# Gathers of the edge passes: a wait before every pair on the pair two back, in place of a wait before every run of four

## The reference

```python
m = jnp.concatenate([hc[row], hc[col]], axis=1)
m = jax.nn.silu(m @ w1 + b1)
m = jax.nn.silu(m @ w2 + b2)
agg = jax.ops.segment_sum(m, row, num_segments=N) * C
```

```python
m_j = norm[:, None] * x[from_]
out = jax.ops.segment_sum(m_j, to_, num_segments=n)
```

## Time and profile before

| | |
|---|---|
| median of 3 runs | 12680.3 us (12676.23 to 12695.34) |
| profiled execution | 12673.93 us, its span 12672.1 us |
| POOL busy | 7744.8 us, 61% of the span |
| PE busy | 9185.8 us, 72% |
| DVE busy | 5764.2 us, 45% |
| ACT busy | 2483.4 us, 20% |
| gathers of `edge_messages` (L1210) | 4160, mean 1014 ns |

### The profile page before, as it was taken

How to read it: one execution, slowest core, us unless ns; L and a number is a source line. 1 busy time by engine, 2 the same in 40 slices (tenths; PEclk the granted TensorE clock), 3 DMA queues, 4 the chain that set the end, 5 groups by cost and what they waited for, 6 DMA issues and landing times. The chain is left out here.

```text
span 12672.1 us, 187503 instructions
## 1 busy us (share of the span) xinstructions
PE 9185.8 (72%) x45085; PEld 7667.0 (61%) x45086; DVE 5764.2 (45%) x14751; ACT 2483.4 (20%) x4616; POOL 7744.8 (61%) x7547
## 2 busy tenths in 40 slices
PE   3774488777887777777777777999996667774333
PEld 2663244466766666566666666888885556664333
DVE  9773000034333333333333334888888733333223
ACT  0000233300011000100010001555554611110000
POOL 5556777666655666566656664555553456665776
PEclk5555689866666666666666666999998967775555
DMA  1332244421113111311121112888886412221111
GB/s 28 101 109 67 85 145 138 125 48 44 43 37 73 44 43 44 66 43 44 43 57 43 44 43 77 254 254 253 254 253 169 127 48 51 52 51 28 25 25 25
DMA packets 854760, 1110.03 MB, mean 88 GB/s; under 512 B 337331, under 2 KB 531544, under 8 KB 853398
## 3 DMA queue, kind: packets, MB, share of 16 engines
q1 hardware_dynamic: 306058, 473.67, 13.0%
q0 software_dynamic: 264160, 418.34, 12.0%
q10 hardware_dynamic: 284332, 215.58, 6.6%
HBM read 898.41 MB, written 208.50 MB: 87 GB/s over the span
## 5 line engine op out<-in xcount | busy, mean ns | idle before, releaser
L1210 POOL DMA_INDIRECT gx_l<-xr,gi_l x4160 | 4219.5, 1014 | 2475.5 <-DMA gx_l<-xr,gi_l 1155.2
L1332 DVE TENSOR_TENSOR pre_s_l<-psum,gx_l 128x512 f32<-128x512 f32 x520 | 359.7, 692 | 3251.6 <-DMA gx_l<-xr,gi_l 3251.6
L1375 PE MATMUL psum<-ptab,oht 128*128 x6656 | 1288.5, 374 | 405.3 <-issue 333.6
L1375 PEld LDWEIGHTS psum<-ptab,oht 128*128 128x128 f32 x6656 | 1216.1, 282 | 517.7 <-issue 517.7
L1902 PE MATMUL psum<-cw,xa 128*128 128x256 f32 x6656 | 1503.4, 382 | 26.7 <-DVE xa L1988 24.5
L1319 DVE TENSOR_TENSOR aggT_l<-aggT_l,psum 64x128 f32 x4160 | 1157.1, 278 | 755.6 <-DVE aggT_l L1319 724.5
L1890 POOL DMA_INDIRECT gx<-xr,gi x832 | 899.4, 1081 | 969.1 <-DVEq L1979 467.7
L1902 PEld LDWEIGHTS psum<-cw,xa 128*128 128x128 f32 x6656 | 1237.6, 191 | 231.0 <-issue 75.3
L926 POOL DMA_INDIRECT slots_s<-rec_s,row_s x806 | 815.1, 1011 | 590.7 <-issue 339.4
L1223 PE MATMUL psum<-ident,pre_s_l 128*128 128x128 f32 x2080 | 379.2, 312 | 939.2 <-DVE pre_s_l L1332 939.0
L2512 POOL DMA_INDIRECT gx_l<-xr,gi_l x832 | 823.5, 990 | 321.4 <-issue 162.0
(11 more groups left out here) (374 smaller groups left out, 12380.3 us busy)
## 6 DMA issues: line engine op xcount, KB each, us to landing
wkv<-slots_d ACTq DMA_DIRECT2D x208, 568.0 KB, 6.7
kr<-keyrow_s SPq DMA_DIRECT2D x416, 256.0 KB, 3.1
shb<-shT SPq DMA_DIRECT2D x1664, 64.0 KB
gx_l<-xr,gi_l POOLq DMA_INDIRECT x4992, 2.4
vtab<-kv ACTq DMA_DIRECT2D x208, 256.0 KB
v_in<-vtab SPq DMA_DIRECT2D x104, 512.0 KB, 3.5
hT<-noderow SPq DMA_DIRECT2D x101, 512.0 KB
kr<-keyrow_d SPq DMA_DIRECT2D x208, 128.0 KB, 5.4
```

Of the source, the lines that this page charges most:

```text
L1210: pool.indirect_dma_start(gx[j][:, c_, :], None, xr, bass.IndirectOffsetOnAxis(ap=gi[j][:, c_:c_ + 1], axis=0)).then_inc(rows_in[j][h].sem ...
L1375: ins = pe.matmul(bank[0][:, t * D:(t + 1) * D], oht[:, t * P:(t + 1) * P], ptab[:, bass.ds(bl[t // PER["s"]] * D, D)], start=True, stop=True)
```

## The change

The eight gathers of a group now form four pairs (`PAIR = 2`), each with a semaphore of its own. Before every pair POOL waits for the pair two back: before the third and fourth pair for the first and second of the same group, before the first and second pair for the third and fourth of the previous group. DVE's step L1332 waits for four semaphores instead of two. No gather, no transfer and no arithmetic is added or taken away. In the changed kernel the lines behind the declarations are numbered lower, the gather is L1206 and the sum with the gathered rows L1328.

```diff
-            rows_in = [[sig(f"landed{j}_{h}") for h in range(2)] for j in range(AHEAD)]
-            share = [W - W // RUN, W // RUN]
+            rows_in = [[sig(f"landed{j}_{h}") for h in range(W // PAIR)] for j in range(AHEAD)]
...
                         for c_ in range(W):
-                            h = int(c_ % RUN == RUN - 1)
-                            if c_ and c_ % RUN == 0:
-                                pool.wait_ge(rows_in[j][0].sem, rows_in[j][0].n + (k.uses(0, AHEAD) - 1) * (16 * share[0]) + 16 * (c_ - c_ // RUN))
-                                pool.nop(nofuse=True)
-                            elif c_ == 0 and k.has(0, 1):
-                                of = rows_in[k.buf(1, AHEAD)][0]
-                                pool.wait_ge(of.sem, of.n + k.uses(1, AHEAD) * (16 * share[0]))
+                            h = c_ // PAIR
+                            if c_ % PAIR == 0 and (h >= 2 or k.has(0, 1)):
+                                s_, two_back = (0, rows_in[j][h - 2]) if h >= 2 else (1, rows_in[k.buf(1, AHEAD)][h + 2])
+                                pool.wait_ge(two_back.sem, two_back.n + k.uses(s_, AHEAD) * (16 * PAIR))
                                 pool.nop(nofuse=True)
...
-                        for h in range(2):
-                            dve.wait_ge(rows_in[r][h].sem, rows_in[r][h].n + k.uses(3, AHEAD) * (16 * share[h]))
+                        for h in range(W // PAIR):
+                            dve.wait_ge(rows_in[r][h].sem, rows_in[r][h].n + k.uses(3, AHEAD) * (16 * PAIR))
```

More of the change, by code:

```diff
@@ L1355, in edge_messages @@
             for j in range(AHEAD):
-                for h in range(2):
-                    rows_in[j][h].n += 16 * share[h] * len(range(j, n, AHEAD))
+                for h in range(W // PAIR):
+                    rows_in[j][h].n += 16 * PAIR * len(range(j, n, AHEAD))
             for j in range(2):
```

## The result

The changed kernel took 11692.48 us, median of 4 runs (11692.31 to 11718.12), beside 12686.99 us for the kernel before (12676.23 to 12695.34, 4 runs): ratio 0.9221, 95% interval 0.9209 to 0.9233. The forecast was 11924 us in a range of 11810 to 12180. The profiled execution has a span of 11690.6 us, 981.5 less than before.

What follows compares the result with a forecast made beforehand. POOL was taken as the bound, part of its time waiting for gathers to land. Terms 735 + 28 + 3 - 10 = 756 us off 12673.93 gave 11918, plus 6 11924; range 11810 to 12060, upper end 12180 for 8 in 10.

Steps and rivals of the forecast that it cites:

- The waits: POOL's waits for a DMA before gathers fall to the usual 0.30 us each: 756 us less in all.
- L: Landing time, from the end of the awaited gather to the start of the waiting one: 2.24 to 2.51 us.
- slack: Time on POOL from the newest awaited gather's end to the waiting one's earliest start: 2.78 us, more than the landing times.
- The layers' starts: Waits beside bulk loads where the four layers start, 119 us: 28 us go, at most 107.
- The stretching: Gathers lengthened beside DVE's L1308, 0.60 us a group: left unchanged; if it vanished, 312 us more would go.
- the convolution's pace: A milder bound, 0.24 us a group under the forecast's pace, 115 us: the range's lower end, 11810.
- The extra waits: Two more waits per group on POOL and two more semaphores on DVE: cost nothing, on DVE under 50 us.
- PE: Next to late, 10.29 us a group in a layer, 10.91 with features: nothing taken, 27 us kept for the range.
- The lock-out rival: Three DVE steps on SBUF alone hold gathers for their full length, 2.14 us a group: no change, 12680; chance 0.05.
- Later landings: Rival: more transfers in flight, each landing later; at 4.0 us 425 us more, 13100; chance 0.04.

Runs made afterwards that it cites:

- run 4: Changed kernel with DVE's one-hot step `oh` moved ahead of the index copy `gi` and of `oht`: 11945.98 us, ratio 0.9418.
- Run 1: Kernel before, with one constant operand of the one-hot step `oh` read from PSUM instead of SBUF in the four layers: 12676.2 us, ratio 0.999.
- run 3: Changed kernel with runs of four gathers again, each waiting for the same run of the previous group, eight gathers back: 11583.57 us, ratio 0.9133.
- run 9: The changed kernel, unaltered, on the third chip: 14588.31 us, ratio 1.0516 to the kernel before there.
- run 12: Kernel before, one-hot operand in PSUM in the layers and the `kr` load cut to an eighth, on the third chip: 14102.46 us, ratio 1.0123.
- run 8: Changed kernel with every pair waiting for the pair just before it, on the second chip: 17024.49 us, ratio 1.2407.
- run 15: Changed kernel with each gather of the edge passes fetching 64 bytes a row instead of 256, on the fourth chip: 11683.51 us, ratio 0.919.
- runs 5: Kernel before, one-hot operand in PSUM in the layers and the `kr` load cut to an eighth, on the second chip: 13845.15 us, ratio 1.0078.

## Why the prediction was wrong

1. **The waits: right.** Forecast were 756 us, measured are 732 above 0.30 us. L of 2.24 to 2.51 us against a slack of 2.78 explains it in the calm stretches. The layers' starts gave 107 - 76 = 31 us where 28 were taken (96.5 us in 67 waits are left).
2. **The stretching: the step that failed.** It was put as "this is once a group before and after, so I leave the 0.60". Measured are 0.56 us a group before and 0.18 after, 196.5 us less busy time. The step took the number of meetings for their price. The price of one is what is left of the DVE step when the gather starts, less 0.12 us: run 4 moved `oh` and nothing else, and 179 us of busy time came back. Run 1 shows that in the layers the stretching was covered by the wait before the fifth gather as long as that wait was there. The working had named 312 us as the upper bound of this term and left the range's lower end at the convolution's pace, 115 us under the forecast; taking the 312 as the end would have held the time.
3. **A term not seen: 58 us.** Before the change 45 gathers, the second of a group and every 88th of a pass, come 1.67 us after their predecessor with "issue" as the end, 64 us above 0.30 with two others. After it every 84th has a gap of 0.6 to 1.2 us, 27 us above 0.30 in all, and nearly all of these end with a DMA and so are inside the 732. In run 3 there is none. With -6 us at the passes' starts the terms give 732 + 58 + 196 - 6 = 980 us. What the pauses are no run tells.
4. **The extra waits cost nothing: right on POOL, not shown on DVE.** A gather behind a wait that is over starts 0.30 us after its predecessor, as one without a wait does (the rows at 4007.45 and 4005.99). No run takes DVE's two extra waits away alone; run 3 has fewer of them and older transfers to wait for as well.
5. **PE: right, with a miss in the size.** The clock rose, and PE did not become the bound. Its waits for L1328 were to fall under 1 us a group. They are 46.4 / 103 = 0.45 with features but 136.8 / 97.6 = 1.40 in layer 1, because its own time fell with the clock from 10.29 to 10.24 - 1.40 = 8.84 us, more than the period did.
6. **The lock-out rival: wrong in its sum, right in its mechanism.** It said that all three steps would hold gathers for their full length, and a mean above 1.1 us; the mean is 0.967. A gather is held until the end of the step, but it pays only what is left of it, and in the changed kernel few gathers start early in a step. That these steps "already find no gap", which was said against this rival, did not settle it: with no gap the phase still sets the price. The Trainium skill, page "SBUF — State Buffer", section "SBUF: two separate sides", says that GpSimd and a DVE instruction in a two-port mode, or one with two SBUF inputs where the GpSimd operation reads SBUF, lock each other out of a shared port pair for the whole instruction. By that rule, these traces agree: gathers that start inside `oh` end 0.81 to 0.86 us after its end, one was held for 1.09 us of its 1.22 (run 4), and with one operand out of SBUF the gathers beside it are not held (run 1).
7. **Later landings: not on the chips of the first kind**, where the median is 2.4 us. On the third chip the change is slower, the side that this rival stood for, but not by its mechanism: waits for a DMA are 213 us there.

## What to carry to other kernels

When a wait goes, everything that lay beside it changes its price: an overlap that cost nothing inside the wait is paid afterwards. Its size goes with the phase of the two engines: here a gather paid what was left of the DVE step at its start. So put the new pace beside the other engine's steps, or bound the term by zero and by the step's full length. Count how far back the awaited transfer is, in time of the issuing engine, and compare it with the landing time; one more transfer of slack is worth more than more semaphores. Measure such a change on more than one chip.

## What was not expected of the hardware

The sign depends on the chip. In the comparison of the result and on the first, fourth and fifth chip the kernel before takes 12686 to 12721 us, and the changed kernel, where it was run there, 0.9221 and 0.9212 of it. On the two others it takes 13720 and 13905 us, and every version that lets POOL issue with less waiting is 5% slower still, the changed kernel at 1.0516. DVE's idle time without a named end falls with the waiting of POOL: 5656 us in run 9, 5099 in run 12 with the old waits, 1936 in run 8, where POOL waits before every pair. That fits an interference of the issuing of indirect DMAs with the other engines on those chips, and the windows of run 9 show it plainest, in a stage that the change does not touch: DVE does 55 instructions in 200 us beside POOL's scatters and 628 without them, at 1 GB/s. For the 5% of the change it is argued and not shown: no trace of the kernel before exists from such a chip, no run takes the issuing away alone, the run that should tell bytes from issuing in the passes (run 15) landed on a chip of the first kind, and an eighth of the load of `kr` did not help (runs 5 and 12). Why two of the chips behave so is open.

A gather that starts inside `oh`, a DVE step with two SBUF operands, is held until the step ends: it ends 0.81 to 0.86 us after the step, whatever its start, and was stretched by up to 1.09 us (run 4). With one operand in PSUM it is not held. The step `oht`, which reads one tensor of SBUF and writes to SBUF, holds gathers in the same way.
